# A new order of work in the synthesis steps, the hand-over to them and the first image of an attention and filter kernel

## What is computed

```
# layer 0: attention over the n = 1024 points of an image
hn  = group_norm(x); q, k, v = conv1x1(hn)
att = softmax(q.T @ k * c**-0.5);  x1 = x + conv1x1(v @ att.T)
# layer 1: filter in the frequency plane
xf  = fftshift(fft2(x1, norm='ortho'))
center = abs(xf).mean(axis=channels)[7 x 7 middle]      # -> MLP -> 3 parameters
kern   = anisotropic 7 x 7 kernel of these parameters, one for each image
filt   = depthwise 7 x 7 convolution (zero padded) of xf.real and xf.imag
out    = ifft2(ifftshift(wr @ filt), norm='ortho').real + x1
```

## Time and profile before

| | |
|---|---|
| time, median of 3 runs | 448.34 us (446.85 to 448.39) |
| the profiled execution: time, span | 445.73 us, 443.9 us |
| TensorE busy | 423.7 us (95%), 2348 matmuls |
| VectorE, ScalarE, GpSimd busy | 307.6, 249.8, 233.2 us |
| mean granted clock of TensorE | 0.949 |
| attention, to the last scores and features in `image` | to 322 us of the span |
| `last()` | to 348.5 us |
| steps 0 to 6, step 7 and the last store | to 434.5, to 443.9 us |

### The profile page before, as it was taken

One profiled execution on the slowest core, in us unless ns is written; L12 is line 12 of the kernel. 1 busy time (PEld: TensorE's weight loads), 2 busy tenths in 40 slices (PEclk: granted clock), 3 DMA queues, 4 the chain that ended last, 5 costly groups with the idle time before them and its releaser, 6 DMA issues.

```text
span 443.9 us, 7138 instructions
## 1 busy us (share of the span) xinstructions
PE 423.7 (95%) x2348; PEld 354.2 (80%) x2348; DVE 307.6 (69%) x607; ACT 249.8 (56%) x460; POOL 233.2 (53%) x201
## 2 busy tenths in 40 slices
PE   5889999999999999999999999999999889899995
PEld 3667788888888888888888888888878768788884
DVE  3579698678849976884987688487854336674455
ACT  2467676657737665674776667676522344434251
POOL 3097457537825763682576367357531344634362
PEclk9989999999999999999999999999999658888699
DMA  4905100100010010001001000100650001111112
GB/s 115 365 14 232 48 1 1 47 1 0 6 41 0 0 47 0 0 0 47 0 0 47 0 0 0 48 1 1 136 189 1 1 0 48 49 47 49 47 49 95
DMA packets 6385, 19.70 MB, mean 44 GB/s; under 512 B 1664, under 2 KB 2304, under 8 KB 5888
## 3 DMA queue, kind: packets, MB, share of 16 engines
q1 hardware_dynamic: 4240, 12.53, 7.8%
q0 software_dynamic: 688, 6.29, 4.4%
q10 hardware_dynamic: 1440, 0.66, 0.5%
HBM read 15.28 MB, written 4.19 MB: 44 GB/s over the span
## 4 chain that ended last, share of the span: by engine, by line
PE 88%; DVE 4%; ACT 4%; POOL 1%; ACTq 1%; issue 1%; DVEq 0%; POOLq 0%
PE PS L399 66%; PE PS L498 12%; PE PS L551 7%; PE PS L542 2%; PE PS L575 1%; DVE NMX L1249 1%; ACT E L941 1%; DVE ETL L1264 1%; ACTq L887 1%; ACT ETH L950 1%; DVE E L1323 0%; POOL E L1693 0%; DVE XTL L1269 0%; ACT ETH L984 0%; DVE ETL L1291 0%
## 5 line engine op out<-in xcount | busy, mean ns | idle before, releaser
L1693 POOL TENSOR_TENSOR E<-E,RI 128x1024 f32<-128x1024 f32 x64 | 124.6, 1948 | 79.0 <-DVE RI L1254 79.0
L1249 DVE TENSOR_REDUCE NMX<-PS 128x1 f32<-128x1024 f32 x64 | 77.8, 1216 | 34.7 <-PE PS L399 33.9
L399 PE MATMUL PS<-QK 128*128 128x512 f32 x384 | 99.8, 399 | 1.7 <-ACT E L941 1.2
L950 ACT ACTIVATE ETH<-PS 128x512 fp32r<-128x512 f32 x128 | 69.6, 597 | 39.4 <-PE PS L498 39.0
L941 ACT ACTIVATE E<-PS,NMX 128x1024 f32<-128x1024 f32 x64 | 71.5, 1117 | 31.7 <-DVE NMX L1249 31.6
L399 PEld LDWEIGHTS PS<-QK 128*128 128x128 f32 x384 | 70.9, 189 | 17.4 <-ACT E L941 1.7
L1264 DVE TENSOR_TENSOR ETL<-PS,ETH 128x512 fp32r<-128x512 f32 x128 | 81.9, 681 | 3.5 <-ACT ETH L950 2.6
L498 PE MATMUL PS<-MISC,E 128*128 128x128 f32 x512 | 68.0, 276 | 3.0 <-POOL E L1693 2.1
L498 PEld LDWEIGHTS PS<-MISC,E 128*128 128x128 f32 x512 | 59.4, 142 | 13.7 <-POOL E L1693 5.0
L399 PE MATMUL PS<-ETH,VH 128*128 128x512 f32 x128 | 54.5, 426 | 0.0
L399 PE MATMUL PS<-ETH,VL 128*128 128x512 f32 x128 | 50.4, 394 | 0.0
(11 more groups left out here) (196 smaller groups left out, 720.7 us busy)
## 6 DMA issues: line engine op xcount, KB each, us to landing
XTF<-in_xt SPq DMA_DIRECT2D x8, 512.0 KB, 3.3
X<-in_x SPq DMA_DIRECT2D x7, 512.0 KB, 7.1
out<-X SPq DMA_DIRECT2D x7, 512.0 KB, 2.6
QK<-in_gam POOLq DMA_DIRECT2D x1, 1488.4 KB, 9.3
ANH<-in_anh POOLq DMA_DIRECT2D x1, 1320.0 KB, 6.0
ANL<-in_anl POOLq DMA_DIRECT2D x1, 1320.0 KB, 9.8
ETH<-in_syh POOLq DMA_DIRECT2D x1, 1264.0 KB, 6.0
ETL<-in_syl POOLq DMA_DIRECT2D x1, 752.0 KB, 7.1
```

Of the source, the lines that this page charges most:

```text
L399: return pe.matmul(o, a, b_, start=start, stop=stop)
L950: act.activation(et[:, h, 4 * k:4 * k + 4, i * P:(i + 1) * P], bank(ET_BANK + k).rearrange("p (j n) -> p j n", j=4), ACT.Copy).then_inc(s[ ...
L1249: dve.tensor_reduce(NMX[:, t % 2:t % 2 + 1], s_bank(t), AX.X, ALU.max, negate=True)\
L1693: TT(e, e, RI[:, t % 4:t % 4 + 1].broadcast_to([P, N]), ALU.mult)\
```

## The change

Only orders change; no instruction is added, removed or given another size. On TensorE a step becomes `z` 0, `z` 1, `r3`, `khat` 0, `khat` 1, `v3`, `vt`, `rt`, `mix` 0, `mix` 1, with batch 1's small parts at new places among them; ScalarE and VectorE follow in part. In `last()` the four parts of `borders(0, ...)` stand earlier, and the second four features later. In the first image VectorE takes `row_max` of tile 1 ahead of `row_sum` of tile 0, and GpSimd takes the two `value_lo` behind the scalings of tiles 2 and 3.

```diff
--- before.py
+++ after.py
@@ -802,28 +802,28 @@
...
                 values(p, 1, 2, pv=pv)
+                borders(0, 0)
                 x1_transposes(p, 0)
...
                 values(p, 1, 3, pv=pv)
-                borders(0, 0)
+                borders(0, 1)
                 pe.wait_ge(s["v_xl"], 2 * p + 1)
...
                     features(t, o)
-                borders(0, 1)
+                borders(0, 2)
                 out_project(p, 1, False)
-                borders(0, 2)
+                borders(0, 3)
                 khat(0, 0)
...
                 x1_transposes(p, 1)
-                borders(0, 3)
+                pe.wait_ge(s["v_g"], 3)
+                khat(0, 1)
+                v3(0)
+                vt(0)
                 pe.wait_ge(s["v_xl"], 2 * p + 2)
...
                 ins.then_inc(s["p_u"], 1)
-                pe.wait_ge(s["v_g"], 3)
-                khat(0, 1)
-                v3(0)
-                vt(0)
                 rt(1)
...
@@ -831,8 +831,11 @@
...
                 z(i, 0)
+                z(i, 1)
                 if more:
                     r3(i + 1, after_mix=is_later(i))
+                    khat(i + 1, 0)
+                    khat(i + 1, 1)
                 if i == 1:
...
@@ -842,28 +845,25 @@
...
                     borders(1, 0)
-                z(i, 1)
+                if more:
+                    v3(i + 1)
+                if i == 0:
+                    centre(1)
                 if i == 4:
...
                 if more:
-                    v3(i + 1)
-                    khat(i + 1, 0)
-                    khat(i + 1, 1)
+                    vt(i + 1)
                 if i == 0:
-                    centre(1)
+                    hidden(1)
                 if i == 3:
...
                     borders(1, 2)
-                if more:
-                    vt(i + 1)
-                if i == 0:
-                    hidden(1)
+                if more > 1:
+                    rt(i + 2)
                 if i == 4:
...
                 mix(i, 0, last=more == 0)
-                if more > 1:
-                    rt(i + 2)
                 if i == 0:
...
@@ -1090,18 +1090,18 @@
...
                 out_hi(p, 1, LAST_PV_BANK)
+                g_hi(0)
                 khat_copy(0, 0)
...
                 r3_copy(0)
-                misc_hi(XTH[:, 4:8, :], "p_xt", 2 * p + 2, "a_xh")
-                g_hi(0)
                 act.wait_ge(s["g_g3z"], 1)
                 g3_copy(0)
+                misc_hi(XTH[:, 4:8, :], "p_xt", 2 * p + 2, "a_xh")
                 khat_copy(0, 1)
-                features_copy(p, LAST_U_BANK)
                 v3_hi(0)
...
                 g3_copy(1)
+                features_copy(p, LAST_U_BANK)
                 rt_hi(1)
...
@@ -1114,16 +1114,16 @@
...
                     g_hi(i + 1)
-                    r3_copy(i + 1)
                 z_hi(i, 0)
                 if more:
+                    r3_copy(i + 1)
+                z_hi(i, 1)
+                if more:
+                    khat_copy(i + 1, 0)
                     v3_hi(i + 1)
-                z_hi(i, 1)
+                    khat_copy(i + 1, 1)
                 if i == 0:
                     magnitude(1)
-                if more:
-                    khat_copy(i + 1, 0)
-                    khat_copy(i + 1, 1)
                 if i == 1:
...
@@ -1349,8 +1349,10 @@
...
                         dve.tensor_copy(GAO[:], GA[:]).then_inc(s["v_gao"], 1)
-                    if cur:
+                    if cur and (prev or t != 1):
                         row_max(b, t)
+                    if not prev and t == 0:
+                        row_max(b, 1)
                     if not nxt and t == 5:
...
@@ -1585,13 +1587,13 @@
...
                 out_lo(p, 1, LAST_PV_BANK)
-                residual(p, 1)
-                misc_lo(XTL[:, 4:8, :], XTH[:, 4:8, :], "a_xh", 2 * p + 2, "v_xl")
                 g_columns(0)
...
                 g_full(0)
+                residual(p, 1)
                 g3_columns(0)
                 g_lo(0)
+                misc_lo(XTL[:, 4:8, :], XTH[:, 4:8, :], "a_xh", 2 * p + 2, "v_xl")
                 v3_lo(0)
...
@@ -1604,29 +1606,29 @@
...
                     g_lo(i + 1)
+                if i == 2:
+                    mlp_sign(1)
+                z_sum(i, 1)
+                if not more:
+
+                    z_lo_last(0)
+                    z_lo_last(1)
+                if more:
+                    v3_lo(i + 1)
+                if i == 0:
+                    centre_copy(1)
                 if i == 1:
                     params(1)
-                if i == 2:
-                    mlp_sign(1)
                 if i == 3:
                     kernel_of(1)
-                z_sum(i, 1)
-                if not more:
-
-                    z_lo_last(0)
-                    z_lo_last(1)
+                if more > 1 and i != 4:
+                    g_full(i + 2)
                 if i == 0:
-                    centre_copy(1)
+                    hidden_copy(1)
                 if i == 1:
...
                     mlp_angle(1)
-                if more:
-                    v3_lo(i + 1)
-                if more > 1 and i != 4:
-                    g_full(i + 2)
-                if i == 0:
-                    hidden_copy(1)
                 if more:
...
@@ -1729,9 +1731,9 @@
...
                 for t in range(TILES):
-                    if cur and t == (4 if prev else 0):
+                    if prev and cur and t == 4:
                         value_lo(b, 0)
-                    if cur and t == (6 if prev else 1):
+                    if prev and cur and t == 6:
                         value_lo(b, 1)
...
@@ -1744,6 +1746,8 @@
...
                         scale(b, t)
+                    if not prev and t in (2, 3):
+                        value_lo(b, t - 2)
                     if prev and t == 3:
...
```

More of the change, by code:

```diff
@@ L1606, in step @@
                     g_lo(i + 1)
-                if i == 1:
-                    params(1)
                 if i == 2:
                     mlp_sign(1)
-                if i == 3:
-                    kernel_of(1)
                 z_sum(i, 1)
@@ L1617, in step @@
                     z_lo_last(1)
+                if more:
+                    v3_lo(i + 1)
                 if i == 0:
                     centre_copy(1)
+                if i == 1:
+                    params(1)
+                if i == 3:
+                    kernel_of(1)
+                if more > 1 and i != 4:
+                    g_full(i + 2)
+                if i == 0:
+                    hidden_copy(1)
                 if i == 1:
```

## The result

| | before | after |
|---|---|---|
| median of 14 runs each | 446.91 us (441.82 to 449.52) | 449.12 us (448.77 to 451.45) |
| profiled execution: time, span | 445.73, 443.9 us | 449.17, 447.4 us |
| mean granted clock | 0.949 | 0.943 |

The ratio is 1.008 with a 95% interval of 1.0056 to 1.0105: the new order is slower by 0.8%, where no change had been forecast. Every ratio and interval here leaves out the runs that are over 1.5% above the quickest of their kernel (three of before's fourteen, none of after's); the two medians of the table, over all runs, stand only at 1.005. The runs of before lie up to 7.7 us apart.

The account below looks back on a forecast made before the run. TensorE, and the clock it runs at, was taken to bound the kernel. Steps summed to 0.0; +2.25 ahead of them (3.1 - 0.5 - 0.35) took the profiled 445.73 us to 448.0, range 442.5 to 452.5.

Parts of the forecast that it names:

- The low time decides: TensorE sets the end; its clock matters, and two low stretches outweigh every stall together; 44 us low against 41.
- `last`: Hand-over before step 0: clock falls some 6.8 low us sooner, +3.1, and idle time shrinks, -0.5.
- The first image: Attention start: transposes come earlier, but value_lo and two issues delay scale 3 to 32.05; -0.35 taken, bounds 0 and 2.0.
- the table: Steps 0 to 6 worked out from work, stalls and low clock; changes against before sum to 0.0.
- Step 4's number: Step 4: 8.5 work, 3.7 for borders in the narrow row, 4.1 for low clock: 16.3 us, before 14.23.
- The wait at `centre`: Step 0: magnitude moves behind the khat copies, v3_hi and z_hi on ScalarE, so centre waits 2.9 us instead of 1.39.
- The ordinary stall of `vt`: Each step's narrow row: vt waits 0.55 us because v3_hi now follows z_hi 1 on ScalarE; bounds 0 and 1.0.
- 1.56 becomes 0.55 + 0.3 for mlp_sign: Step 2: the old 1.56 us stall shrinks as mlp_angle leaves v3_lo's path; step worked out at 10.95, before 13.03.
- rival (d): Each fall of the clock lasts twice as long; three more stretches of 1.6 give 452.8 us; chance 0.15.
- rival (b): The clock holds in all five plain narrow rows, steps 1, 2, 3, 5 and 6: 440.0 us; chance 0.08.
- the prediction's own test: Steps 5 and 6 at clock 0.50 for part of their row confirm the narrow-row argument; at 1.00 throughout refute it.
- argument on the narrow row: Steps: a narrow row of 4.0 + 0.55 us, half as long again, drops the clock once each, mostly 3.4 us.

Follow-up runs that it names:

- e11: Kernel before with the new step order on TensorE alone, ScalarE and VectorE as before: 454.57 us, ratio 1.0182.
- e12: e2's kernel with unread 512-column matmuls where TensorE stands idle and between step 4's borders parts: 439.19 us, ratio 0.9833 to the kernel before.
- e8: Changed kernel with rt between the two mixes again: 450.23 us, ratio 1.0098 to the kernel before.
- e9: Changed kernel with e5's and e7's edits together and VectorE's small chain (mlp_sign, mlp_size, mlp_angle) moved: 447.93 us, ratio 1.0029 to the kernel before.
- e2: Kernel before with only the new order of last(), steps and first image as before: 444.54 us, ratio 0.9955.
- e3: Kernel before with only the two new orders in the first image: 446.01 us, ratio 1.0006.
- e5: Changed kernel with step 0's magnitude on ScalarE directly behind z_hi 1: 446.47 us, ratio 1.0017 to the kernel before.
- e4: Changed kernel with step 2's mlp_sign behind v3_lo instead of ahead of z_sum 1 on VectorE: 449.66 us, ratio 1.0069 to the kernel before.
- e1: Kernel before with only the new order of the synthesis steps on TensorE, ScalarE and VectorE: 450.26 us, ratio 1.0102.
- e7: Changed kernel with the first two borders parts of step 4 between and behind the two z: 446.29 us, ratio 1.0023 to the kernel before.

## Why the prediction failed

*The low time decides.* Right in the main: the longest span is that with the most low time (e11, 452.1 us with 51.2) and the shortest that with the least (e12, 436.6 with 13.7). But it isn't all: e8 and e9 have 47.8 us each, and spans of 449.1 and 446.0.

*`last`.* Right in mechanism, and in size partly by luck. Forecast 3.1 - 0.5 = 2.6 us later; e2, which has this part alone, is 2.61 later. But image 1's normalised rows came 0.32 us earlier in e2 (40.67 for 40.99), so the part itself costs 2.93. Its two terms were both too small: ahead of z(0, 0) e2 has 8.5 low us more than before, not 6.8, and its waits there are 0.94 us instead of 1.91, 0.97 less and not 0.5. In after z(0, 0) is 1.33 later instead of 2.25, because the first image, seen at image 1's normalised rows, was 1.66 earlier; 1.01 of that stood already at the first row_max (17.94 us for 18.95), ahead of all that the change moves. The wait for residual is 0.93 where 1.2 was forecast.

*The first image.* Right in mechanism. GpSimd after:

```profile
28.57 1.27 POOL L1681 TENSOR_TENSOR VL<-XTF,VH 128x512 fp32r<-128x512 f32 x1
29.78 0.78 POOL L1754 DMA_DIRECT2D ANH<-in_anh  x1
...
31.11 1.92 POOL L1695 TENSOR_TENSOR E<-E,RI 128x1024 f32<-128x1024 f32 x1
```

value_lo and the two issues stand ahead of scale 3, as forecast: 31.11 with the 1.01 of the start is 32.12, forecast 32.05, before 32.46. e3 measures no gain. Counted from the first row_max, the normalised rows of image 1 come 0.65 us sooner in after and 0.66 in e3, where 0.35 was taken.

*The steps.* By the table: step 0 15.0 for 15.9, step 1 11.17 for 10.75, step 3 11.59 for 11.1, step 4 16.34 for 16.3, step 5 10.67 for 10.65, step 6 9.85 for 10.3. Step 4's number is right with a wrong reason: its few columns were said to mind the clock little, but 16 matmuls of 2 columns take 0.86 us at the full clock (before, 409.16) and 1.49 at the low (after, 410.87). The wait at `centre` was put at 2.9 and is 2.72; e5 shows that it matters. ScalarE's queue ahead of it in after's timeline, the last khat copy, the table load, the magnitude:

```profile
354.91 0.58 ACT L979 ACTIVATE E<-PS 128x512 f32<-128x512 f32 x1
355.51 1.28 ACT L1062 ACT_TABLE_LOAD   x1
...
356.91 0.23 ACT L1065 ACTIVATE R<-R 128x50 f32<-128x50 f32 x1
```

The ordinary stall of `vt` was put at 0.55 and is 0.18 in steps 5 and 6. Step 1 has no fall of its own; in its place z(2, 0) waits 1.13 us for `vt_lo`, held up behind `mlp_size` on VectorE (L1463 alone takes 1.24 us).

**The first step that failed** is step 2: "1.56 becomes 0.55 + 0.3 for mlp_sign". The step took 13.26 us, not 10.95, the wait grew to 2.06, and the fall lasted 6.8 us instead of 3.4. The 0.3 was a price of small operations by themselves; the row measured 1.6 us from 379.46 to 381.04, since one of them ran for as long as GpSimd's. The trace before had the same price to be read, in the very wait of 1.56 us: the last operation of mlp_angle, then v3_lo, and GpSimd's z_lo beside them, from before's timelines:

```profile
383.56 1.14 DVE L1510 TENSOR_TENSOR ML<-ML 49x2 f32<-49x2 f32 x1
384.74 0.29 DVE L1291 TENSOR_TENSOR ETH<-PS,ETH 64x128 fp32r<-64x128 f32 x1
...
383.42 1.27 POOL L1724 TENSOR_TENSOR ETL<-E,ETH 128x512 fp32r<-128x512 f32 x1 [0.80 <-ACT ETH L984]
```

So about 1 us of the old wait was this one operation too, and the change put another in its place. e4 shows the step's excess to be this, and also that curing it alone doesn't make the kernel faster. In sum the table is 1.9 us short, and with the earlier z(0, 0) and the longer step 7 the forecast change against the profiled execution, +2.25, became +3.47 in the span. The low time was put at 44 us and is 47.8 in the profiled execution: the forecast's rival (d), longer falls, came true in step 2 and in `last` (10.2 against "6.8 low us sooner"), in no other.

**The second** is "I put its median at 448.0". The sum was a difference, +2.25 us to one execution, and was set as a level beside a median of three runs, 448.34. Fourteen runs put before's median at 446.91. The difference added to that gives 449.16, and 449.12 was measured. Read as a difference the forecast was +0.5%, just on the bound between no change and slower, and just below the measured interval, which begins at 0.56%; "forecast: no change" came from the level. That the two agree to 0.04 us is partly luck, since step 2 and z(0, 0) erred in opposite directions in a single execution.

*The clock holds in the plain narrow rows*, rival (b): refuted in this form by steps 3, 5 and 6 of after, which fell with 0.09, 0.18 and 0.18 us idle. Here the Trainium skill ("TensorE: Matmul & The Clock Gate", "Why this matters for your kernels") names idle gaps between bursts of matmuls as what to avoid. The runs agree as far as stalls go: those of 0.9 to 2.3 us filled with wide work (e12 against e2) give back 1.2%. They disagree in that the rows of steps 3, 5 and 6 fell almost without a gap.

**What stays open.** Which low stretch comes in a given run is not settled: those of steps 5 and 6 came in after, e4, e8 and e9 and not in e1, e5 and e7, with the same instructions in the step. By the prediction's own test the first four confirm its argument on the narrow row and the last three refute it. So e5 and e7 show that their edits pay, but not that the cause ends in the step where they are made. The share of the narrow row and of the stall in step 3 was not separated.

## What to carry to other kernels

Where an engine's clock can fall, price an order by what stands between wide matmuls, stalls first, and test it by filling the stalls with unread wide work: that gave 1.2% here in two kernels, more than any order did, and in the third 0.8% at most. Give a sum worked out from one execution as a difference, and add it to a median of many runs. Before moving a small operation ahead of one that the path waits for, look at what other engines run at that moment, and follow the chain to the next step, where the gain of e4 was lost.

## What was not expected of the hardware

A VectorE operation of 49 x 2 numbers in SBUF, 0.15 us by itself, takes 1.14 to 1.25 us when it meets a running GpSimd operation on SBUF of 128 x 512: L1494 1.25 us beside `z_lo`'s 1.27, L1501 1.22 beside `k_x1`, and before's L1510 1.14. With the chain moved to where GpSimd is idle, e9's timeline of VectorE has

```profile
378.00 0.16 DVE L1494 TENSOR_SCALAR ML<-ML 49x2 f32<-49x2 f32 x1
```

The v3_lo above, which reads PSUM, takes its 0.29 us beside GpSimd. The Trainium skill ("GPSIMD Engine Reference", "8. Key points") says that the two engines share their SBUF interfaces and contend for some kinds of VectorE instructions; the trace agrees and adds the price, about the remaining length of GpSimd's instruction. The second surprise is the size of e12: 24 matmuls that nobody reads take e2's ratio of 0.9955 to 0.9833, some 5.5 us.
